# First experts: weights stream past stationary tokens in rounded products, and the latent softmax finishes in PSUM

## What is computed

```python
x = x + L0_xattn(layernorm(x), ctx)      # masked linear attention: Q + tril(K K^T) Q
x = x + L0_ffn(layernorm(x), ...)        # latent attention, 16 heads of 8, then 8 experts, top 2
x = x + L1_xattn(layernorm(x), ctx, ...) # cross attention, 16 heads of 64, softmax
x = x + L1_ffn(x, ...)                   # 16 experts, top 2, and a shared expert

# the part of L0_ffn that the change is about
t = rmsnorm(x, g2)
hid = silu(t @ w1[e]) * (t @ w3[e])      # 256 -> 512, for the two chosen experts e
y_e = hid @ w2[e]                        # 512 -> 256
# and in its attention
attn = softmax(scores, axis=-1); o = attn @ v
```

## Time and profile before

| | us |
|---|---|
| the profiled execution | 937.17 |
| its span, first to last instruction | 935.4 |
| median of three runs | 941.88 |
| TensorE busy | 868.6 (93%) |
| VectorE busy | 714.8 (76%) |
| ScalarE busy | 604.1 (65%) |
| GpSimd busy | 291.1 (31%) |

### The profile page before, as it was taken

How to read it: one execution, slowest core, us unless ns; L and a number is a source line. 1 busy time by engine, 2 the same in 40 slices (tenths; PEclk the granted TensorE clock), 3 DMA queues, 4 the chain that set the end, 5 groups by cost and what they waited for, 6 DMA issues and landing times.

```text
span 935.4 us, 23731 instructions
## 1 busy us (share of the span) xinstructions
PE 868.6 (93%) x7932; PEld 781.7 (84%) x7932; DVE 714.8 (76%) x1945; ACT 604.1 (65%) x1694; POOL 291.1 (31%) x359
## 2 busy tenths in 40 slices
PE   5898888867999999999899999999998999999997
PEld 3775555536999999998789998989887989999996
DVE  4778999874767666675899888986777637888867
ACT  4478787854666666675677667776876326777740
POOL 3845676651000000002623346221112103445430
PEclk9999999999999999999999999999999999999999
DMA  8239310241111111133101122021006952333335
GB/s 307 103 115 430 123 35 25 115 169 63 52 52 53 52 52 52 53 125 130 45 15 36 35 92 86 19 81 57 2 24 250 407 110 82 99 96 101 97 117 197
DMA packets 43032, 97.12 MB, mean 104 GB/s; under 512 B 6080, under 2 KB 28480, under 8 KB 41504
## 3 DMA queue, kind: packets, MB, share of 16 engines
q1 hardware_dynamic: 36048, 76.80, 23.6%
q0 software_dynamic: 6864, 18.80, 5.8%
HBM read 62.21 MB, written 33.37 MB: 102 GB/s over the span
## 4 chain that ended last, share of the span: by engine, by line
PE 78%; DVE 12%; issue 4%; POOL 2%; DMA 2%; ACT 2%; SPq 0%; DVEq 0%; POOLq 0%; ACTq 0%
PE ps L915 24%; PE ps L734 11%; PE ps L736 10%; PE ps L735 10%; PE ps L1002 4%; PE ps L1012 3%; PE ps L1026 3%; PE ps L1084 2%; DVE BIG L1476 2%; PE ps L852 1%; PE ps L900 1%; PE ps L901 1%; PE ps L867 1%; PE ps L803 1%; DMA small<-in_small 1%
## 5 line engine op out<-in xcount | busy, mean ns | idle before, releaser
L734 PE MATMUL ps<-BIGR 128*128 128x256 f32 (+1 forms) x826 | 257.6, 312 | 5.2 <-DVE BIGR L1735 2.3
L915 PE MATMUL ps<-BIG 128*128 128x128 f32 x2000 | 252.2, 276 | 0.5 <-issue 0.5
L915 PEld LDWEIGHTS ps<-BIG 128*128 128x128 f32 x2000 | 238.7, 193 | 0.8 <-issue 0.7
L736 PE MATMUL ps<-BIGR 128*128 128x256 f32 x778 | 220.9, 284 | 0.0
L735 PE MATMUL ps<-BIGR 128*128 128x256 f32 (+1 forms) x602 | 176.8, 294 | 0.0
L734 PEld LDWEIGHTS ps<-BIGR 128*128 128x128 f32 x826 | 156.7, 190 | 12.3 <-issue 7.2
L736 PEld LDWEIGHTS ps<-BIGR 128*128 128x128 f32 x778 | 147.2, 189 | 0.7
L1222 ACT COPY BIG<-BIG 128x512 f32 (+1 forms) x86 | 70.1, 815 | 107.0 <-PE ps L915 99.7
L735 PEld LDWEIGHTS ps<-BIGR 128*128 128x128 f32 x602 | 114.4, 190 | 1.6
L1708 DVE TENSOR_TENSOR BIGR<-BIG,BIGR 128x512 fp32r<-128x512 f32 (+1 forms) x86 | 80.8, 940 | 37.2 <-ACT BIGR L1231 37.1
L1980 POOL DMA_INDIRECT BIG<-ys_dram,YI x32 | 33.9, 1059 | 225.7 <-DMA ys_dram<-BIG 217.3
(11 more groups left out here) (237 smaller groups left out, 1806.0 us busy)
## 6 DMA issues: line engine op xcount, KB each, us to landing
BIG<-in_wgu SPq DMA_DIRECT2D x2, 6144.0 KB, 25.8
BIG<-in_wd SPq DMA_DIRECT2D x2, 4096.0 KB, 22.7
BIG<-xs_dram SPq DMA_DIRECT2D x47, 129.5 KB, 2.1
xs_dram<-CT SPq DMA_DIRECT2D x8, 640.0 KB, 4.2
BIG<-xs_dram SPq DMA_DIRECT2D x39, 128.0 KB, 2.0
ys_dram<-BIG SPq DMA_DIRECT2D x39, 128.0 KB, 1.7
BIG<-in_wkv SPq DMA_DIRECT2D x2, 2048.0 KB, 9.9
kv_dram<-BIG SPq DMA_DIRECT2D x16, 256.0 KB, 2.0
```

What stands on the lines that cost most here:

```text
L734: pe.matmul(o, l[0], r[0], start=start, stop=False)
L736: return pe.matmul(o, l[1], r[0], start=False, stop=stop)
L915: i = pe.matmul(o[:, c * 128:(c + 1) * 128], wt[:, at:at + 128], x[:, k * 128:(k + 1) * 128], start=k == 0, stop=k == 1)
```

## The change

- **gate and up** of the first experts: the tokens become the stationary operand and the weights the moving one, 512 columns at a time, in three rounded products (`rows_through`). The weights come in pieces: four per tile (gate and up, two halves of the 256 channels each), in a ring of five (`PIECES`). `wp` on ACT makes a piece's high part and multiplies by g2, `wl` on DVE its low part. `xTh` and `xTl` do the same for the transposed tokens
- the result has the tokens on partitions, so `hT` transposes the hidden values with four products into PSUM bank 7; `hh` and `hTl` read them from there
- **the low part of the down weights** moves from DVE (`wdl`) to GpSimd (`wdp`), in two halves of 512 columns
- the buffers: rows and results have two in place of three, the hidden values one in place of two
- **the latent stage**: `nrm0` transposes from PSUM to the free half of the same bank and reads the products' inputs from there, and the bank is given back after the products; `tt` moves from DVE to ACT and no longer multiplies by g2
- the work array of `places` moves to the space that `load_kv` fills, and `load_kv` waits for it
- the planner's durations of the latent phases and all of `LEAD` are new, and with them the order of the queues. The list of `LEAD` is left out here, as are the latent durations. In the second experts (r = 1) nothing changes but names

```diff
...
+PIECES = 5
...
+LATE = {"DVE": 170, "POOL": 90}
...
-        add("DVE", 550, ("tt", b), ("pow3", b), ("sc", 0, b - 3))
...
+        add("ACT", 290, ("tt", b), ("pow3", b), ("sc", 0, b - 3))
...
-    nd, ny = ((1, 3), (2, 3))[r]
+    nd, ny = ((1, 2), (2, 3))[r]
     for j in range(NT_[r]):
         def add(engine, ns, name, *after, banks=(), **kw):
             p.add(engine, ns, (name, r, j), *after, banks=[(ring + str(r), (q, r, j)) for ring, q in banks],
                   due=3 * j, **kw)
         begin = start if j == 0 else []
-        add("SP", 1000, "xs", ("xT", r, j - 3), *([("ix", r, j - 3)] if r else []), *begin, late=28000 if r and j < 3 else 2200)
-        add("ACT", 100 + 0.84 * n, "wa", ("up", r, j - 2), *begin)
-        add("DVE", 60 + 0.6 * n, "wv", ("up", r, j - 2), *begin)
+        add("SP", 1000, "xs", ("xT", r, j - (2, 3)[r]), *([("ix", r, j - 3)] if r else []), *begin, late=28000 if r and j < 3 else 2200)
         add("ACT", 100 + 0.84 * n, "wdh", ("down", r, j - nd), *begin)
-        add("DVE", 70 + 1.04 * n, "wdl", ("wdh", r, j))
-        add("PE", 220, "xT", ("xs", r, j), banks=[("xT", "xT_e")])
-        add("ACT", 270, "xT_e", ("xT", r, j), ("up", r, j - 2))
-        add("PE", 3.52 * F, "gate", ("xT_e", r, j), ("wv", r, j), ("wa", r, j), banks=[("gate", "silu")])
-        add("PE", 3.52 * F, "up", ("gate", r, j), banks=[("up", "hm")])
-        add("ACT", 62 + 0.79 * F, "silu", ("gate", r, j), ("hl", r, j - 2))
-        add("DVE", 70 + 1.04 * F, "hm", ("up", r, j), ("silu", r, j))
-        add("ACT", 90 + 0.84 * F, "hh", ("hm", r, j), ("down", r, j - 1))
-        add("DVE", 70 + 1.04 * F, "hl", ("hh", r, j))
-        add("PE", 2.82 * F, "down", ("hl", r, j), ("wdl", r, j), banks=[("down", "y")])
+        if r == 0:
+            for i in range(4 * j, 4 * j + 4):
+                before = [("up" if (i - PIECES) % 4 > 1 else "gate", 0, (i - PIECES) // 4)] if i >= PIECES else []
+                p.add("ACT", 450, ("wp", 0, i), *before, *begin, due=3 * j)
+                p.add("DVE", 640, ("wl", 0, i), ("wp", 0, i), due=3 * j)
+            add("POOL", 2150, "wdp", ("wdh", r, j), ("down", r, j - nd))
+            add("PE", 220, "xT", ("xs", r, j), banks=[("xT", "xTl")])
+            add("ACT", 270, "xTh", ("xT", r, j), ("up", r, j - 2))
+            add("DVE", 300, "xTl", ("xTh", r, j), ("up", r, j - 2))
+            add("PE", 1400, "gate", ("xTl", r, j), ("wl", 0, 4 * j + 1), banks=[("gate", "silu")])
+            add("PE", 1400, "up", ("gate", r, j), ("wl", 0, 4 * j + 3), banks=[("up", "hm")])
+            add("ACT", 430, "silu", ("gate", r, j), ("hT", r, j - 1))
+            add("DVE", 570, "hm", ("up", r, j), ("silu", r, j))
+            add("PE", 437, "hT", ("hm", r, j), banks=[("hT", "hTl")])
+            add("ACT", 500, "hh", ("hT", r, j), ("down", r, j - 1))
+            add("DVE", 570, "hTl", ("hh", r, j))
+        else:
...
+        add("PE", 2.82 * F, "down", *([("hl", r, j), ("wdl", r, j)] if r else [("hTl", r, j), ("wdp", r, j)]), banks=[("down", "y")])
...
-    p.add("SP", 100, ("load_kv",), ("xT", 0, 6), due=0, late=12000)
+    p.add("SP", 100, ("load_kv",), ("xT", 0, 6), ("places",), due=0, late=12000)
...
-         "xT0": (0,), "gate0": (1, 4), "up0": (2, 5), "down0": (3, 6),
+         "xT0": (0,), "gate0": (1, 4), "up0": (2, 5), "down0": (3, 6), "hT0": (7,),
...
-        W_ = [ex0.ring(2, 4 * F0)]
+        W_ = [ex0.ring(PIECES, 2 * F0, r=True)]
         WDN_ = [Space((96, 104)).ring(1, 4 * F0, r=True)]
-        XS_, XT_, H_ = [ex0.ring(3, D)], [ex0.ring(2, D)], [ex0.ring(2, F0)]
-        HT_, Y_ = [ex0.ring(1, 2 * F0, r=True)], [ex0.ring(3, D)]
+        XT_, HT_ = [ex0.ring(2, 2 * D, r=True)], [ex0.ring(1, 2 * F0, r=True)]
+        XS_, H_ = [ex0.ring(2, D)], [ex0.ring(1, F0)]
+        Y_ = [ex0.ring(2, D)]
...
-        OHW = [big(152, 2 * NB * E_[i], pat="p (a n) -> p a n", n=E_[i]) for i in range(2)]
+        OHW = [big((104, 152)[i], 2 * NB * E_[i], pat="p (a n) -> p a n", n=E_[i]) for i in range(2)]
...
+            def rows_through(j, which):
+                o, x = ps(which, 0, j), XT_[0][j % 2]
+                vacant(pe, which, 0, j)
+                if which == "gate":
+                    pe.wait_ge(*emptied("xT", 0, j))
+                for k in range(2):
+                    i = 4 * j + (2 if which == "up" else 0) + k
+                    w = W_[0][i % PIECES]
+                    pe.wait_ge(*done("wl", 0, i))
+                    m = mm3(pe, o[:, :], [x[:, h * D + k * 128:h * D + k * 128 + 128] for h in range(2)],
+                            [w[:, 0:F0], w[:, F0:2 * F0]], k == 0, k == 1)
+                m.then_inc(*fills(which, 0, j))
+            def hT(_, j):
+                vacant(pe, "hT", 0, j)
+                pe.wait_ge(*emptied("up", 0, j))
+                for c in range(F0 // 128):
+                    at = slice(c * 128, c * 128 + 128)
+                    i = pe.transpose(ps("hT", 0, j)[:, at], H_[0][0][:, at], ident)
+                i.then_inc(*fills("hT", 0, j))
             def gate_up(r, j, which):
+                if r == 0:
+                    return rows_through(j, which)
...
-                pe.wait_ge(*done("hl", r, j))
-                pe.wait_ge(*done("wdl", r, j))
+                pe.wait_ge(*(done("hl", r, j) if r else emptied("hT", 0, j)))
+                pe.wait_ge(*done("wdl" if r else "wdp", r, j))
...
+            def tt(b):
+                act.wait_ge(*done("pow3", b))
+                if b >= 3:
+                    act.wait_ge(sem(f"scattered{tile_of(0, b)}"), 32 * len([n for n in range(b) if tile_of(0, n) == tile_of(0, b)]))
+                act.mul(TT[tile_of(0, b)][:, 0:D], r_[b % 2][:, 0:D], rstd[:, b:b + 1]).then_inc(S["tokens_ready"], 1)
...
+            def piece(e, i):
+                return WGU[:, bass.ds(e * (4 * F0) + i % 2 * 2 * F0 + i % 4 // 2 * F0, F0)], g2c[:, i % 2:i % 2 + 1]
+            def wp(_, i):
+                if i == 0:
+                    act.wait_ge(sem("tiles_listed"), 1)
+                    act.wait_ge(sem("wgu_loaded"), 32)
+                    latent_over(act)
+                if i >= PIECES:
+                    act.wait_ge(*full("up" if (i - PIECES) % 4 > 1 else "gate", 0, (i - PIECES) // 4))
+                w, gain = piece(expert_of(0, i // 4), i)
+                act.mul(W_[0][i % PIECES][:, 0:F0], w, gain).then_inc(S["weights_by_act"], 1)
+            def xTh(_, j):
+                act.wait_ge(*full("xT", 0, j))
+                if j >= 2:
+                    act.wait_ge(*full("up", 0, j - 2))
+                act.copy(XT_[0][j % 2][:, 0:D], ps("xT", 0, j)[:, 0:D]).then_inc(S["operand_hi"], 1)
...
-                sums = ot_.rearrange("p (c r) -> p c r", r=32)
+                o = ps("pv", b)
+                sums = o[:, 256:512].rearrange("p (c r) -> p c r", r=32)
                 v.wait_ge(*full("pv", b))
-                v.transpose(ot_, ps("pv", b)[:, 0:256]).then_inc(*frees("pv", b))
-                v.wait_ge(*emptied("pv", b))
+                v.transpose(o[:, 256:512], o[:, 0:256]).then_inc(dv, next_step("dve"))
+                then()
                 v.reciprocal(sr_.rearrange("p (c j) -> p c j", c=8), sums[:, :, 16:18]).then_inc(dv, next_step("dve"))
                 then()
                 for x in range(2):
@@ -1488,8 +1568,9 @@
                     v.tensor_tensor(on_.rearrange("p (c x j d) -> p c x j d", c=4, x=2, j=2)[:, :, x, :, :],
                                     sums[:, at, 0:16].rearrange("p c (j d) -> p c j d", j=2),
                                     sr_.rearrange("p (c j o) -> p c j o", c=8, o=1)[:, at, :, :].broadcast_to([128, 4, 2, 8]),
-                                    ALU.mult).then_inc(dv, next_step("dve"))
-                then()
+                                    ALU.mult).then_inc(*(frees("pv", b) if x else (dv, next_step("dve"))))
+                then()
+                v.wait_ge(*emptied("pv", b))
...
+            def wl(_, i):
+                v.wait_ge(*done("wp", 0, i))
+                e, w = expert_of(0, i // 4), W_[0][i % PIECES]
+                v.scalar_tensor_tensor(out=w[:, F0:2 * F0],
+                                       in0=WGU[:, bass.ds(e * (4 * F0) + i % 2 * 2 * F0 + i % 4 // 2 * F0, F0)],
+                                       scalar=g2c[:, i % 2:i % 2 + 1], in1=w[:, 0:F0].bitcast(F32), op0=ALU.mult,
+                                       op1=ALU.subtract).then_inc(S["weights_by_dve"], 1)
+            def xTl(_, j):
+                x = XT_[0][j % 2]
+                v.wait_ge(*done("xTh", 0, j))
+                v.tensor_tensor(x[:, D:2 * D], ps("xT", 0, j)[:, 0:D], x[:, 0:D].bitcast(F32),
+                                ALU.subtract).then_inc(*frees("xT", 0, j))
+            def hTl(_, j):
+                h = HT_[0][0]
+                v.wait_ge(*done("hh", 0, j))
+                v.tensor_tensor(h[:, F0:2 * F0], ps("hT", 0, j)[:, :], h[:, 0:F0].bitcast(F32),
```

(10 more changed lines are left out.)

180 lines of the change are left out of this document (96 added, 84 removed), and 16 rows, old and new, of the table LEAD.

## The result

The changed kernel takes 1004.47 us (median of 4 runs, 1003.82 to 1005.18), the kernel before 940.29 us beside it (4 runs, 936.79 to 942.03): a ratio of 1.0704, 95% interval 1.0682 to 1.0725. The profiled execution has a span of 1002.5 us against 935.4, so 67.1 us have to be found.

A forecast was written before the change was run, and what follows sets the result against it. TensorE was taken to bound the experts and VectorE the latent stage; after the change, the loop through the single down-weight buffer. 937.2 + 55 (experts) - 8 (latent) = 984 us, range 935 to 1010.

The forecast's parts named there:

- rival 2: Expert tile: two port turns, or `hh` ahead of `wdh` on ScalarE; 7.2 us a tile, 1004 us; chance 0.12.
- The loop: First experts: down, `wdh`, `wdp` and the next down close through one down-weight buffer; 6.17 us, 6.67 with a port turn.
- hop and register read: Loop, from `wdh`'s end to GpSimd's start: 0.09 us, plus 0.63 us for reading the expert's number into a register.
- the pair: Loop: GpSimd's two 512-column subtractions (`wdp`) for the low down weights, 2.5 us together, bounds 2.05 and 2.6.
- the turn: Loop: a waiting `wl` takes the shared port between GpSimd's two subtractions, 0.5 us, bounds nothing and 1.1.
- Rival 1: Expert loop without the port's turn, or with cheap GpSimd halves: 6.17 us a tile, 965 us (variants 967, 948); chance 0.25.
- rival 3: Experts: TensorE stays the bound, so the kernel gets faster: 916 us, or about 925 when nearly so; chance 0.15.
- The upper bound's 1.1 us: Loop: port delay if a `wl` is also just under way when GpSimd's first half starts; sum then +78 us.
- VectorE's list: Experts: VectorE's operand work per tile, 4.3 us, said to fit tightly within TensorE's 4.88 us.
- The latent term: Latent stage: `tt` leaves VectorE and `onrm` loses its port waits, 1.0 us per block; taken as -8 us, at most 10.
- The order elsewhere: Other stages, cross attention too: the planner's new leads change the order, between -5 and +5 us, taken as nothing.
- The head of the experts: First expert tile: weights needed through `wp` and `wl` before its rows arrive, covered by the row-load wait; no cost.

The follow-up runs named there:

- a1: The changed kernel with GpSimd's register read moved ahead of its wait for `wdh`: 992.9 us beside 954.9 for the kernel before.
- a4: The changed kernel with VectorE making only 32 of 512 columns of each `wl` from the sixth piece on: 1008.3 us beside 954.9 for the kernel before.
- a2: The changed kernel with `wdp` as one GpSimd instruction of 1024 columns in place of two of 512: 992.3 us beside 954.9 for the kernel before.
- a3: The changed kernel with the early register read and `wdp` as one 1024-column instruction: 985.7 us beside 954.9 for the kernel before.
- b1: The changed kernel with two buffers for the split down weights, key and value weights loaded later: ratio 1.0511 to the kernel before.
- c1: The kernel before with the latent edits and, for the latent stage alone, the change's order table, slack and durations: 924.83 us, 0.9859 of before.
- b3: The kernel before with only the latent edits, in the old order, g2 applied to the first experts' transposed tokens: ratio 1.0118 to the kernel before.
- d1: The changed kernel with the kernel before's order and PSUM banks for all work behind the first experts: 990.54 us, ratio 1.0562 to the kernel before.

## Why the prediction was right, and where not

Predicted 984, range 935 to 1010, slower; measured 1004.47, slower. The direction and the mechanism held; the middle was 20 us too low. That rival 2 was priced at 1004 is a coincidence: it had a tile of 7.2 us, and 6.76 was measured.

**The loop, right.** Link by link, predicted and measured: end of down to `wdh` 0.29 and 0.30; `wdh` 1.05 and 1.05; hop and register read 0.09 + 0.63 = 0.72 and 0.74, which by `a1` are 0.19 and 0.55, so that two small misses cancel; the pair 2.5 and, without a turn, 2.53 (`a4`); the turn 0.5 and 0.48; to down 0.10 and 0.15; down 1.51 and 1.51. Together 6.67 and 6.76. The 1.26 us for a 512-column subtraction, read off a line through 256 and 1024 columns, was 1.26 to 1.31. Rival 1 (no turn, or cheap halves) and rival 2 (two turns) fall by the same numbers, and rival 3 (TensorE stays the bound) with them. The spread of the two lines of the port, in the change between 260 and 430 us:

```profile
L2091 POOL TENSOR_TENSOR BIGR<-BIG,BIGR x52: 1274/1312/1771, 258.7 to 428.7; 128x512 fp32r<-128x512 f32 x52
...
L1781 DVE SCALAR_TENSOR_TENSOR BIGR<-BIG,small,BIGR x102: 735/746/1759, 259.8 to 429.2; 128x512 fp32r<-128x512 f32 x102
```

In each pair one instruction takes some 1.3 us and the other 1.77; and `wl` runs from 0.74 to 1.76, as the prediction's last part wanted (a tail to 1.9).

**The port rule.** The prediction weighed a rule of the Trainium skill, "SBUF — State Buffer", section "Who interferes with whom": who issues first keeps the port for the whole instruction. `a2` and `a3` agree with it from both sides, GpSimd first and then VectorE first, with 1.1 and 0.49 us of waiting. It holds for one instruction, not for a run of them: the change's pair was entered in its middle. In the settled tiles of the change no `wl` was under way when the pair began. In `a1` and `a3` one was, once the pair came earlier, but then none came in the middle. The upper bound's 1.1 us wants both in one pair; that is seen in `b1` alone, where the median half takes 1.74 us.

**VectorE's list, too short.** The prediction had 4.3 us a tile and therefore took TensorE's 4.88 as the floor. Its eight instructions take 4 x 0.74 + 0.69 + 0.68 + 0.41 + 0.41 = 5.15 us undisturbed, 4.5 with the overlap of 0.08 each, since `wl` costs 0.74 and not 0.68. (In the same way ScalarE's `wp` took 0.72 and not 0.61 us, which the prediction had allowed for and which stayed off the path.) The larger miss: the port was counted for what it does to GpSimd's pair, never for what it does to VectorE, 1.0 us a tile in the change (`wl` at 1.00 in the mean) and 1.2 in `b1`. Together that is the 5.7 us of `b1`, and the 5.85 of the change (23.37 of 27 us in the stretch above) but for 0.3. It did not change the forecast, since the loop was longer, but rival 3, priced at 916 us, could not have come with every link short, and its chance of 0.15 was too high.

**The latent term, right in sign, half of its cause missing.** -8 was predicted and -12.0 came. The prediction said: VectorE's list gets shorter, so the stage does, and the order is worth nothing. VectorE's list did get shorter (54.3 to 50.0 us in the stretch of `c1`), but `b3` shows no gain from the same edits in the old order; the order had to be made anew for them. That the number came near is in part luck. The waits themselves went as predicted; the products of `onrm`, in place of 209/224/1541 ns:

```profile
L1568 DVE TENSOR_TENSOR BIG<-ps,BIG x32: 214/220/225, 54.8 to 192.5; 128x64 f32<-128x64 f32 x32
```

**The order elsewhere, wrong.** It was taken as 0, between -5 and +5, and cost 14.2 us behind the experts, of which `d1` gives 10.9 back. This is the term that moved the middle of the forecast.

**The head of the experts, wrong.** "Covered by the wait for the row load" did not hold: +4.4 us. From the timeline of the first tile:

```profile
206.22 2.93 POOL L2091 TENSOR_TENSOR BIGR<-BIG,BIGR 128x512 fp32r<-128x512 f32 x2 [3.90 <-ACT BIGR L1308]
206.89 3.48 DVE L1781 SCALAR_TENSOR_TENSOR BIGR<-BIG,small,BIGR 128x512 fp32r<-128x512 f32 x3 [3.81 <-ACT BIGR L1280]
210.29 0.41 DVE L1789 TENSOR_TENSOR BIGR<-ps,BIGR 128x256 fp32r<-128x256 f32 x1
...
210.80 0.77 PE L756 MATMUL ps<-BIGR 128*128 128x512 f32 x1 [4.42 <-DVE BIGR L1789]
```

GpSimd makes its down half first, though nobody needs it yet; three `wl` stand behind it, `xTl` (line 1789) behind them, and TensorE waits 4.42 us for that one. The port was costed only inside the loop. It explains part of the wait: of the three `wl` the first takes 1.15 and the second 1.75 us in place of 0.74, 1.4 us in all. More time goes behind the wait, to TensorE's clock. In the settled stage it is granted in full (1.00, the level of 2.4 GHz). From 210.5 to 214 us, after the 4.42 us of waiting, the granted clock is 0.50 (1.2 GHz), and the products of lines 756 to 758 start 0.43 us apart and not 0.23. The kernel before has such a stretch too, at 0.59 between 219 and 223 us.

At the other end of the stage VectorE's first splits of the key weights (line 1830, 1.83 and 2.29 us in place of 1.22) get into the last pair and hold it up, so that it takes 3.48 us; TensorE waits 5.03 us for it and then makes the last down product at a granted clock of 0.51, its products 0.21 us apart in place of 0.12. The two stretches:

```profile
210.50:214.00 3.50, 3.20 (x9) 2.54 (x10) 1.52 (x3) 0.17 (x1) 0.00 (x0) 0.50 0.00 0
478.70:482.00 3.30, 3.27 (x15) 3.30 (x16) 1.30 (x2) 0.00 (x0) 0.00 (x0) 0.51 0.00 0
```

Neither end was tried by itself, so how the 4.4 us divide is argued and not shown.

In sum: +5.6 in the experts (0.09 us a tile, and the last tiles), +4.4 at the head, +14.2 behind, -4.0 in the latent stage, that is 20.2 of the 20.5 us between 984 and 1004.5.

## What to carry over

A buffer without a second copy makes a loop of everything from its last reader back to it, and its length is a sum of links that can be read off a trace, even for an engine that never did the work: a line through two sizes of the same operation, and the price of a register read from another engine. Handing work to an idle engine paid nothing here, because the work lay inside such a loop and its engine shares a port with the one that it was to relieve; both are to be checked first. And where a planner lays the order, an edit and its order are one thing: neither the latent edits nor the order alone was worth having here, together they gave 1.4%; and where an order is laid anew for one stage, keep the old one behind it, or measure what the new one costs there (10.9 us here).
